# A recommender tower on one core: the first stage rearranged, and three lookups of the second quarter done ahead of the first product

## The chip, the cores and the metric

The kernel runs on one core of a Trainium2 chip. The metric is the device time of one execution in microseconds (us). The engines are TensorE (PE, with its weight loads shown apart as PEld), VectorE (DVE), ScalarE (ACT), GpSimd (POOL) and SyncE (SP), which here only issues transfers. ACT, SP and POOL issue transfers too; those issues are shown as ACTq, SPq and POOLq.

## The reference

2048 samples. For each sample 16 rows of 16 numbers are looked up in 16 tables (e), and there is an input r_x0 of 39 x 16. Their interaction is compressed to 16 x 16 numbers, and three dense layers follow:

```
e = stack([tbl_s[ids[:, s]] for s in range(16)], axis=1)          # 2048 x 16 x 16
A  = repeat(r_x0, 16, axis=1)                                     # 2048 x 624 x 16
Bm = repeat(e, 39, axis=2).reshape(2048, 624, 16)
z  = einsum('bnh,bnd,nk,khd,kd->bkh', A, Bm, alpha, w, hv)        # 2048 x 16 x 16
h  = concat([z.reshape(2048, 256), dense_ctx])                    # 272 values
y  = relu(relu(h @ W1 + b1) @ W2 + b2) @ W3                       # 2048 x 1
```

What matters here is that the product of A and Bm needs every sample's looked-up rows, and that alpha, w and hv combine to constant coefficients that don't depend on the sample.

## The kernel before, in words

**Groups.** The samples are worked on in 8 groups of 256. For each group, ACT copies the looked-up rows into a wide layout (spread, L401), TensorE transposes it into PSUM (transpose_values, L657), VectorE multiplies it with r_x0 in five products of 128 x 2048 (L576), TensorE contracts each product with the coefficients (contract, L667), and the three dense layers of the group run on TensorE beside the next group's products (layer1 L682 and L688, layer2 L698, layer3 L707) with ACT applying the nonlinearities.

**Lookups.** Seven tables are gathered by POOL with indirect transfers (L322, 14 per group). The nine small tables are looked up with matmuls: their row number is split into a low and a high digit; VectorE compares the low digit with a column of numbers (make_onehot, L524), TensorE multiplies the one-hot matrix with the table, which is split into three bf16 parts (look_up, L627, 24 matmuls; the first three tables of the nine have 64 columns, the other six 80), and VectorE picks the row by the high digit and sums (pick_rows, L536 and L540). A unit is one table for one quarter of the samples (512, two groups). Units 0 to 8 are the first quarter, done in the prologue; units 9 to 17, the second quarter, are spread over groups 0 and 1 by units_at: two beside group 0's first product, then one, one, two, one, and one beside each of group 1's first two. One-hot matrices cover half of the samples, so units 9 to 17 use those of units 0 to 8, and units 18 to 35 need the second half's digits.

**Prologue.** SP loads the row numbers, the small tables, masks, alpha, a slot mask and the weights (L272 to L278). VectorE finds the digits; ACT stores the low digits to memory (L374) and loads them back, replicated over the partitions, in three transfers (low_h, L333). VectorE makes the pick mask (L489), multiplies alpha with a mask (spread_alpha, L507), splits the tables (L496 to L502) and multiplies the weights (L514). TensorE sums alpha over the slots (sum_alpha, L595); ACT spreads the weights and the sums into block layouts (L344, L350 to L356); TensorE makes the coefficients (make_coef, L608 and L610, for each k of 16: four small matmuls into c_ps, one into c4_ps); ACT copies them to SBUF (copy_coef, L366 and L368). In program order TensorE does sum_alpha, nine lookups, with one make_coef behind each from the fourth on, the remaining ten make_coef, and then the transposes of group 0. A float32 product shows as two matmuls in the records, so make_coef has 8 + 2.

**Dense inputs.** dense_ctx and its layer weights are loaded in four replicas by 12 transfers (L297, L298) into the not yet used second half of x0_last and into z_sb, rounded by ACT (round_dense, L384, L385) and reduced to their remainders by VectorE (split_dense, L466, L469), which stands behind the third product of group 0. Only after that may x0_last of group 1 be loaded (L288 waits for dense_low).

**What sets the order.** Each engine has one list of instructions, written out by hand, and semaphores between them. All loads named so far except low_h are in SP's list, which first waits for the digits to be in (L292), then issues x0 of group 0, dense, the layers' weights, and x0 of the later groups, each when its buffer is free.

## Time and profile before

| | |
|---|---|
| median of 3 runs | 206.78 us (206.12 to 207.69) |
| the profiled execution's own time | 207.17 us |
| its span, first to last instruction | 205.4 us |
| PE busy | 171.9 us (84%) |
| DVE busy | 149.0 us (73%) |
| POOL busy | 113.2 us (55%) |
| ACT busy | 65.1 us (32%) |
| mean granted TensorE clock | 0.950 |
| pick mask (L489), one instruction | 907 ns |
| weights multiplied (L514) | 425 ns |
| dense rounded (L384 x2, L385) | 2.0 + 0.6 us |
| x0 of a group, loaded | 2 x 512 + 1024 KB |
| dense and w1d, loaded | 8 x 128 + 4 x 64 KB |
| digits (low_h), loaded per half | 3 x 768 KB |

Times in the rows are from the span's start. The page names a group of instructions by line, engine and operation; the timeline gives start and duration, merged where the same instruction repeats, and in brackets the idle time of the engine before it with what ended it. "issue" is time in which the engine waited for nothing that the profile shows. The granted clock is 1.00 at 2.4 GHz and 0.50 at 1.2 GHz. Matmuls are pipelined, so the duration of a merged row overlaps the next by some hundredths of a microsecond.

### The profile page before, as it was taken

The numbers are of one execution on the slowest core, as the hardware profiler recorded it, in microseconds if no ns is written. First come the engines' busy times: TensorE is split into PE (matmuls) and PEld (weight loads), VectorE is DVE, ScalarE is ACT, GpSimd is POOL, SyncE is SP. The second block draws the span as 40 slices with busy tenths as digits, with TensorE's granted clock in tenths as the row PEclk, the third lists the DMA queues.
The fourth block names the chain that finished last, engine by engine and source line by source line (L and its number), as shares of the span: only waits on it lengthen the run. The fifth ranks groups of instructions, "written<-read, shape, count | busy, mean of one in ns | idle before, by whom it ended". The sixth has DMA issues, their size and how long they took to land.

```text
span 205.4 us, 5054 instructions
## 1 busy us (share of the span) xinstructions
PE 171.9 (84%) x2170; PEld 128.2 (62%) x2170; DVE 149.0 (73%) x171; ACT 65.1 (32%) x203; POOL 113.2 (55%) x119
## 2 busy tenths in 40 slices
PE   0318958998638899999967999999899899899983
PEld 0307947896425677677845677777577467477671
DVE  3798872109999979898899968866979595595000
ACT  2098000729300118216201271181117317311322
POOL 2687777777777777777777777777750000000000
PEclk9999995558996999999999999999999999999999
DMA  6495999999837992991039819800693790000000
GB/s 199 146 305 156 218 205 201 271 181 267 214 77 143 197 207 27 214 199 21 6 70 199 164 26 229 175 13 10 155 206 65 184 222 6 0 3 0 3 0 2
DMA packets 11698, 26.63 MB, mean 130 GB/s; under 512 B 3836, under 2 KB 6396, under 8 KB 9628
## 3 DMA queue, kind: packets, MB, share of 16 engines
q1 hardware_dynamic: 5356, 20.50, 45.2%
q10 hardware_dynamic: 2688, 4.76, 7.7%
q0 software_dynamic: 3632, 1.06, 4.6%
q8 instruction: 17, 0.28, 0.6%
q14 instruction: 5, 0.04, 0.1%
HBM read 26.26 MB, written 0.05 MB: 128 GB/s over the span
## 4 chain that ended last, share of the span: by engine, by line
PE 59%; DVE 26%; issue 9%; DMA 2%; ACT 1%; SPq 1%; ACTq 0%; DVEq 0%
DVE prod L576 14%; PE bank L667 13%; PE bank L688 13%; PE bank L698 12%; PE bank L627 10%; PE bank L610 4%; DVE picked L536 4%; DVE onehot L524 3%; PE bank L682 2%; PE bank L657 2%; DMA prod<-slot_mask 2%; PE bank L608 2%; DVE dense_sb L466 1%; DVE prod L498 1%; PE bank L707 1%
## 5 line engine op out<-in xcount | busy, mean ns | idle before, releaser
L322 POOL DMA_INDIRECT e_all<-tbl,ids_sb x112 | 111.7, 998 | 37.6 <-issue 33.8
L576 DVE TENSOR_TENSOR prod<-x_main,bank 128x2048 f32<-128x2048 f32 x32 | 72.2, 2279 | 17.9 <-PE bank L657 9.1
L667 PE MATMUL bank<-prod,coef 128*32 128x256 f32 x640 | 43.5, 391 | 9.0 <-DVE prod L576 8.9
L627 PE MATMUL bank<-parts,onehot 125*128 125x80 bf16 (+1 forms) x864 | 39.6, 211 | 11.6 <-DVE onehot L524 5.6
L627 PEld LDWEIGHTS bank<-parts,onehot 125*128 125x128 bf16 x864 | 37.3, 108 | 15.8 <-issue 6.0
L401 ACT ACTIVATE spread<-e_all 128x128 f32<-128x128 f32 (+3 forms) x128 | 29.0, 329 | 17.5 <-DVE e_all L540 17.2
L667 PEld LDWEIGHTS bank<-prod,coef 128*32 128x32 f32 x640 | 17.0, 110 | 23.4 <-DVE prod L576 12.7
L688 PE MATMUL bank<-z_sb,w1z_sb 128*128 128x256 f32 x128 | 30.3, 380 | 0.0
L698 PE MATMUL bank<-h_sb,w_sb 128*128 128x256 f32 x128 | 29.8, 386 | 0.7 <-ACT h_sb L411 0.7
L698 PEld LDWEIGHTS bank<-h_sb,w_sb 128*128 128x128 f32 x128 | 23.7, 190 | 6.9 <-ACT h_sb L411 3.1
L536 DVE TENSOR_TENSOR picked<-bank,pick 128x320 f32<-128x320 f32 (+1 forms) x36 | 16.7, 465 | 15.2 <-PE bank L627 15.1
L411 ACT ACTIVATE h_sb<-bank 128x512 f32<-128x512 f32 x16 | 9.6, 598 | 53.7 <-PE bank L688 53.7
L688 PEld LDWEIGHTS bank<-z_sb,w1z_sb 128*128 128x128 f32 x128 | 23.1, 189 | 2.7 <-ACT z_sb L431 0.2
L576 DVE TENSOR_TENSOR prod<-x_last,bank 128x2048 f32<-128x2048 f32 x8 | 18.2, 2278 | 0.0
L540 DVE TENSOR_REDUCE e_all<-picked 128x64 f32<-128x320 f32 (+1 forms) x36 | 16.7, 464 | 1.2
L524 DVE TENSOR_SCALAR onehot<-low_h,masks_sb 125x1024 bf16<-125x1024 f16 x36 | 16.2, 497 | 0.0
L657 PEld LDWEIGHTS bank<-ident,spread 128*128 128x128 f32 x80 | 9.5, 155 | 9.5 <-issue 9.5
L657 PE MATMUL bank<-ident,spread 128*128 128x128 f32 x80 | 15.1, 311 | 0.0
L419 ACT ACTIVATE h_sb<-bank,b_sb 128x256 f32<-128x256 f32 x16 | 6.7, 471 | 12.9 <-PE bank L698 12.9
L425 ACT ACTIVATE y_sb<-bank 128x64 f32<-128x64 f32 x8 | 1.8, 224 | 25.9 <-PE bank L707 25.9
L595 PE MATMUL bank<-prod 128*128 128x128 f32 x10 | 2.5, 434 | 8.4 <-DVE prod L507 8.4
L431 ACT ACTIVATE z_sb<-bank 128x512 f32<-128x512 f32 x8 | 4.7, 592 | 14.4 <-PE bank L667 14.4
(41 smaller groups left out, 77.2 us busy)
## 6 DMA issues: line engine op xcount, KB each, us to landing
x_main<-x_m SPq DMA_DIRECT2D x16, 512.0 KB
x_last<-x_l SPq DMA_DIRECT2D x8, 1024.0 KB
low_h<-low_dram ACTq DMA_DIRECT2D x6, 768.0 KB, 8.7
e_all<-tbl,ids_sb POOLq DMA_INDIRECT x112
x_last<-dense_t SPq DMA_DIRECT2D x8, 128.0 KB
prod<-small_tables SPq DMA_DIRECT2D x1, 672.0 KB, 4.6
w1z_sb<-w1z SPq DMA_DIRECT2D x1, 512.0 KB, 14.3
w_sb<-w SPq DMA_DIRECT2D x1, 512.0 KB, 14.3
```

Source lines behind the costliest of these rows:

```text
L322: pool.indirect_dma_start(out=e_all[:, t * E + s * D:t * E + (s + 1) * D], out_offset=None, in_=tables[s], in_offset=bass.IndirectOffsetOn ...
L401: last = act.activation(dst, src, ACT.Copy)
L411: act.activation(h1_sb[:, 2 * i:2 * i + 2, :], h1_ps[i][:, :].rearrange("p (a b) -> p a b", a=2), ACT.Relu).then_inc(h1_ready, 1)
L524: dve.tensor_scalar(onehot[:, n, c, :], low_h[0:RC, n, :], low_sb[:, c:c + 1], None, ALU.is_equal).then_inc(onehot_ready, 1)
L536: dve.tensor_tensor(found, look_ps[i % 2][:, 0:QT * q * D].rearrange("p (t d q) -> p t d q", t=QT, q=q), pick[:, at:at + QT, 0:q].unsqueez ...
L540: dve.tensor_reduce(e_all[:, :].rearrange("p (t i) -> p t i", i=E)[:, u * QT:(u + 1) * QT, s * D:(s + 1) * D], found, AX_X, ALU.add).then_ ...
L576: dve.tensor_tensor(prod[:, c, :, :], x0[:, p, :, :], value_bank(g, c // 2)[:, c % 2 * GB:(c % 2 + 1) * GB].unsqueeze(1).broadcast_to([P, ...
L627: last = pe.matmul(look_ps[i % 2][:, t * w:(t + 1) * w], onehot[:, n, c, at:at + P], parts[:, part, col:col + w], start=(t == 0 and c == 0 ...
L657: last = pe.transpose(value_bank(g, i)[:, col:col + P], spread[:, p, t, c * P:(c + 1) * P], ident[:, :])
L667: last = pe.matmul(z_ps[p][32 * q:32 * q + 32, a * GB:(a + 1) * GB], coef[:, c, 4 * a + q, :], prod[:, c, 4 * a + q, :], start=(c == 0 and ...
L688: last = pe.matmul(out[a], w1z_sb[:, k, cols[a]], z_sb[:, p, k, :], start=False, stop=(k == 1), skip_group_check=True)
L698: last = pe.matmul(out[a], w2_sb[:, c, cols[a]], h1_sb[:, c, :], start=(c == 0), stop=(c == N1 // P - 1))
```

## The change

- SP's first loads are reordered: masks, weights, alpha, slot mask, and the small tables last.
- The loads of low_h move from ACT's list to SP's; the second half's stand behind x0 of group 1 instead of behind round_dense on ACT.
- The dense loads stand ahead of x0 of group 0; round_dense on ACT stands ahead of the spread of group 0, and split_dense on VectorE behind the first quarter's lookups, ahead of the first product.
- VectorE multiplies the weights first, then spreads alpha, then makes the pick mask, then splits the tables.
- make_coef is cut in two: main_coef (c_ps) and last_coef (c4_ps). TensorE makes eight main parts ahead of the first lookup, one behind each of the other eight, and two last parts behind each lookup from the fourth on, the remaining four behind the ninth.
- Units 9, 10 and 11 are looked up and picked ahead of group 0's first product instead of in group 0.

```diff
--- before.py
+++ after.py
@@ -98,9 +98,10 @@
 
 RUNS = spread_runs()
 FIRST_COLS = COL0[3]
-COEF_FROM, DENSE_AT = 3, 2
+COEF_FROM = 3
 
 UNITS_AT = (2, 1, 1, 2, 1, 1, 1)
+AHEAD = 3
 LAYER1_AT, LAYER2_AT = (0, 1), 2
 
 
@@ -109,7 +110,8 @@
     first, at = NSMALL * (step // (2 * NC) + 1), step % (2 * NC)
     if first >= 4 * NSMALL or at >= len(UNITS_AT):
         return range(0)
-    return range(first + sum(UNITS_AT[:at]), first + sum(UNITS_AT[:at + 1]))
+    done = max(AHEAD, sum(UNITS_AT[:at])) if step < 2 * NC else sum(UNITS_AT[:at])
+    return range(first + done, first + max(done, sum(UNITS_AT[:at + 1])))
 
 
 def gathered_by(g):
@@ -270,12 +272,21 @@
         @block.sync
         def _(sp):
             sp.dma_start(ids_i, ids_d).then_inc(digits_in, 16)
-            sp.dma_start(table_sb, small_tables).then_inc(table_in, 16)
             sp.dma_start(masks_sb[:, :], masks).then_inc(masks_in, 16)
+            sp.dma_start(w_hv_sb[:, :], w_hv.unsqueeze(0).broadcast_to([J, D, K * H + K])).then_inc(coef_in, 16)
             sp.dma_start(alpha_sb[:, :, :], alpha.rearrange("(c p) k -> p c k", p=P)).then_inc(prep_in, 16)
             sp.dma_start(mask_sb, slot_mask).then_inc(prep_in, 16)
-
-            sp.dma_start(w_hv_sb[:, :], w_hv.unsqueeze(0).broadcast_to([J, D, K * H + K])).then_inc(coef_in, 16)
+            sp.dma_start(table_sb, small_tables).then_inc(table_in, 16)
+
+            def load_low(a, n, count):
+
+                sp.dma_start(low_h[:, n:n + count, :], low_dram[n:n + count, a * HALF:(a + 1) * HALF].unsqueeze(0).broadcast_to(
+                    [P, count, HALF])).then_inc(low_in[n // 3], 16)
+
+            sp.wait_ge(low_stored, 16)
+            for n in range(0, NSMALL, 3):
+                load_low(0, n, 3)
+
             def load_x0(g, p):
 
                 if g >= 2:
@@ -290,16 +301,20 @@
 
             for n in range(NSMALL // 3):
                 sp.wait_ge(low_in[n], 16)
-            load_x0(0, 0)
             for q in range(4):
                 rows = slice(32 * q, 32 * q + 32)
                 for a in range(2):
                     sp.dma_start(dense_f[a][rows, :], dense_t[:, a * HALF:(a + 1) * HALF]).then_inc(dense_in, 16)
                 sp.dma_start(w1d_f[rows, :], w1d).then_inc(dense_in, 16)
+            load_x0(0, 0)
             sp.dma_start(w1z_sb[:, :, :], w1z.rearrange("(a p) n -> p a n", p=P)).then_inc(mlp_in, 16)
             sp.dma_start(w2_sb[:, :, :], w2.rearrange("(a p) n -> p a n", p=P)).then_inc(mlp_in, 16)
             sp.dma_start(w3_sb[:, :], w3).then_inc(mlp_in, 16)
-            for g in range(1, GROUPS):
+            load_x0(1, 1)
+            sp.wait_ge(onehot_ready, 2 * NSMALL)
+            for n in range(0, NSMALL, 3):
+                load_low(1, n, 3)
+            for g in range(2, GROUPS):
                 load_x0(g, g % 2)
             sp.wait_ge(y_ready, GROUPS)
             sp.dma_start(y.rearrange("(g q b) a -> q g (b a)", g=GROUPS, q=4), y_sb[0:97:32, :, :]).then_inc(stored, 16)
@@ -327,11 +342,6 @@
         @block.scalar
         def _(act):
 
-
-            def load_low(a, n, count):
-
-                act.dma_start(low_h[:, n:n + count, :], low_dram[n:n + count, a * HALF:(a + 1) * HALF].unsqueeze(0).broadcast_to(
-                    [P, count, HALF])).then_inc(low_in[n // 3], 16)
 
             act.wait_ge(warm_ready, 1)
             act.activation(warm[:, 1:2], warm[:, 0:1], ACT.Copy)
@@ -361,7 +371,7 @@
 
             def copy_coef():
 
-                act.wait_ge(c_done, 1)
+                act.wait_ge(c_done, 2)
                 for h in range(2):
                     act.activation(coef[:, 0:MC, :, h * K:(h + 1) * K].rearrange("p c a k -> p (c a) k"),
                                    c_ps[:, :].rearrange("p (k c) -> p c k", k=K), ACT.Copy, scale=half_sb[:, h:h + 1])
@@ -372,9 +382,6 @@
 
             act.wait_ge(low_ready, 1)
             act.dma_start(low_dram.rearrange("n b -> (n b)").rearrange("(p c) -> p c", p=P), low16[:, :]).then_inc(low_stored, 16)
-            act.wait_ge(low_stored, 16)
-            for n in range(0, NSMALL, 3):
-                load_low(0, n, 3)
             spread_weights()
             spread_sums()
 
@@ -431,13 +438,10 @@
                 act.activation(z_sb[:, p, :, :], z_ps[p][:, :].rearrange("p (a b) -> p a b", a=2),
                                ACT.Copy).then_inc(z_ready, 1)
 
+            round_dense()
             act.wait_ge(pads_done, 1)
             spread_group(0, 0)
             copy_coef()
-            round_dense()
-            act.wait_ge(onehot_ready, 2 * NSMALL)
-            for n in range(0, NSMALL, 3):
-                load_low(1, n, 3)
             for g in range(GROUPS):
                 p = g % 2
                 for c in range(NC):
@@ -544,12 +548,12 @@
             find_digits()
             pads = spread[:, :, :, MC * P:EXW].rearrange("p a t (h c) -> p (a t) h c", h=2)
             dve.memset(pads[:, :, :, (F - FM) * J - 1:64], 0.0).then_inc(pads_done, 1)
+            multiply_weights()
+            spread_alpha()
             make_pick()
-            spread_alpha()
             dve.wait_ge(table_in, 16)
             split_tables(0, slice(0, FIRST_COLS))
             dve.wait_ge(split_step, 4)
-            multiply_weights()
             split_tables(1, slice(FIRST_COLS, W))
             make_onehot(0)
             dve.wait_ge(pick_ready, 1)
@@ -558,6 +562,9 @@
                 if n < NSMALL - 1:
                     make_onehot(n + 1)
                 pick_rows(n)
+            split_dense()
+            for i in range(NSMALL, NSMALL + AHEAD):
+                pick_rows(i)
             for i in units_at(0):
                 if i // NSMALL % 2 == 0:
                     make_onehot(i)
@@ -571,14 +578,12 @@
                     if g > 0:
                         dve.wait_ge(contracted, NC * (g - 1) + (c + 1))
                     if g == 0 and c == 3:
-                        dve.wait_ge(c_done, 1)
+                        dve.wait_ge(c_done, 2)
                     x0 = x0_main if c < MC else x0_last
                     dve.tensor_tensor(prod[:, c, :, :], x0[:, p, :, :],
                                       value_bank(g, c // 2)[:, c % 2 * GB:(c % 2 + 1) * GB].unsqueeze(1).broadcast_to(
                                           [P, HP, GB]), ALU.mult).then_inc(product_ready, 1)
 
-                    if g == 0 and c == DENSE_AT:
-                        split_dense()
                     for i in units_at(NC * g + c):
                         pick_rows(i)
                     for i in units_at(NC * g + c + 1):
@@ -596,17 +601,18 @@
                                      alpha_block[:, c, :, :].rearrange("p f k -> p (f k)"), start=True, stop=True)
                 last.then_inc(bsum_done, 1)
 
-            def make_coef(k):
-
-                if k == 0:
-                    pe.wait_ge(bsum_copied, 2)
-                    pe.wait_ge(wblock_done, 1)
-                    pe.wait_ge(blast_done, 1)
+            def main_coef(k):
+
                 for j in range(2):
                     for odd in range(2):
                         row = 64 * j + 32 * odd
-                        pe.matmul(c_ps[row:row + FM, k * MC * HP:(k + 1) * MC * HP], bsum_sb[:, 0:FM, k],
-                                  wblock[:, k, j::2, odd::2], start=True, stop=True)
+                        last = pe.matmul(c_ps[row:row + FM, k * MC * HP:(k + 1) * MC * HP], bsum_sb[:, 0:FM, k],
+                                         wblock[:, k, j::2, odd::2], start=True, stop=True)
+                if k == K - 1:
+                    last.then_inc(c_done, 1)
+
+            def last_coef(k):
+
                 last = pe.matmul(c4_ps[:, k * H:(k + 1) * H], blast[:, k, :, :, :].rearrange("p h f j -> p (h f j)"),
                                  wh_sb[:, k, :], start=True, stop=True)
                 if k == K - 1:
@@ -629,18 +635,29 @@
                                              stop=(c == 1 and part == PARTS - 1), skip_group_check=True)
                 last.then_inc(onehot_used, 1)
 
+            sum_alpha()
+            pe.wait_ge(bsum_copied, 2)
+            pe.wait_ge(wblock_done, 1)
+            for k in range(K - NSMALL + 1):
+                main_coef(k)
+            pe.wait_ge(split_step, 4)
             made = 0
-            sum_alpha()
-            pe.wait_ge(split_step, 4)
             for n in range(NSMALL):
                 if n == 3:
                     pe.wait_ge(split_step, 8)
                 look_up(n)
+                if n > 0:
+                    main_coef(K - NSMALL + n)
+                if n == COEF_FROM:
+                    pe.wait_ge(blast_done, 1)
                 if n >= COEF_FROM:
-                    make_coef(made)
-                    made += 1
+                    for k in range(made, made + 2):
+                        last_coef(k)
+                    made += 2
             for k in range(made, K):
-                make_coef(k)
+                last_coef(k)
+            for i in range(NSMALL, NSMALL + AHEAD):
+                look_up(i)
 
             def transpose_values(g, i):
```

## Rows read from the trace of the kernel before

**Rows 1.** Chain of waits, 24 to 46 us: start, duration, what.
```profile
24.53 0.27 PE bank L608 x8
24.80 0.33 PE bank L610 x2
...
28.46 3.23 issue
...
43.27 0.29 PE bank L608 x7
43.55 0.54 PE bank L610 x2
```

**Rows 2.** Transfer queues, 28 to 30 us: queue, packets, MB, share of 16 engines.
```profile
q8 instruction: 1, 0.02, 3.9%
```

**Rows 3.** Windows: length, PE, PEld, DVE, ACT, POOL busy, PEclk, DMA share, GB/s.
```profile
30.00:40.00 10.00, 8.31 (x115) 7.52 (x115) 1.96 (x4) 3.00 (x13) 7.55 (x8) 0.56 1.06 227
40.00:50.00 10.00, 9.91 (x135) 8.31 (x136) 3.93 (x6) 5.41 (x14) 7.56 (x8) 0.59 1.00 211
```

**Rows 4.** Timeline of TensorE: start, duration, instruction, idle before.
```profile
15.33 2.72 PE L627 MATMUL bank<-parts,onehot 125*128 125x64 bf16 x48 [4.42 <-DVE onehot L524]
...
24.98 1.02 PE L627 MATMUL bank<-parts,onehot 125*128 125x80 bf16 x24
...
34.07 1.76 PE L627 MATMUL bank<-parts,onehot 125*128 125x80 bf16 x24
...
44.30 0.61 PE L610 MATMUL bank<-wh_sb,prod 128*128 128x16 f32 x2
44.75 1.95 PE L657 MATMUL bank<-ident,spread 128*128 128x128 f32 x8
...
62.25 1.93 PE L667 MATMUL bank<-prod,coef 128*32 128x256 f32 x16 [1.68 <-DVE prod L576]
```

**Rows 5.** Timeline of VectorE.
```profile
7.46 0.82 DVE L507 TENSOR_TENSOR prod<-alpha_sb,masks_sb 128x640 f32<-128x640 f32 x1
...
14.30 1.67 DVE L524 TENSOR_SCALAR onehot<-low_h,masks_sb 125x1024 bf16<-125x1024 f16 x4
...
36.40 0.49 DVE L540 TENSOR_REDUCE e_all<-picked 128x64 f32<-128x320 f32 x1
45.98 2.29 DVE L576 TENSOR_TENSOR prod<-x_main,bank 128x2048 f32<-128x2048 f32 x1 [9.10 <-PE bank L657]
...
49.87 2.28 DVE L576 TENSOR_TENSOR prod<-x_main,bank 128x2048 f32<-128x2048 f32 x1
...
55.16 2.36 DVE L466 TENSOR_TENSOR dense_sb<-x_last,dense_sb 64x1024 fp32r<-64x1024 f32 x2
57.56 1.40 DVE L469 TENSOR_TENSOR w1d_sb<-z_sb,w1d_sb 32x512 fp32r<-32x512 f32 x2
...
67.14 2.28 DVE L576 TENSOR_TENSOR prod<-x_main,bank 128x2048 f32<-128x2048 f32 x1
```

**Rows 6.** Timeline of ACT.
```profile
10.77 3.30 ACT L344 ACTIVATE prod<-wh_sb,masks_sb 128x256 f32<-128x256 f32 x8 [8.53 <-DVE wh_sb L514]
...
37.00 3.62 ACT L401 ACTIVATE spread<-e_all 128x128 f32<-128x128 f32 x16 [17.22 <-DVE e_all L540]
...
49.40 3.62 ACT L401 ACTIVATE spread<-e_all 128x128 f32<-128x128 f32 x16 [0.26 <-DMA e_all<-tbl,ids_sb]
...
170.86 3.61 ACT L401 ACTIVATE spread<-e_all 128x128 f32<-128x128 f32 x16
```

**Rows 7.** Timeline of SP's issues.
```profile
18.32 1.15 SPq L285 DMA_DIRECT2D x_main<-x_m  x2
...
26.35 0.44 SPq L299 DMA_DIRECT2D w1z_sb<-w1z  x1
```

**Rows 8.** Issues by line, section 6: count, KB each, us from issue to landing.
```profile
w1z_sb<-w1z SPq DMA_DIRECT2D x1, 512.0 KB, 14.3
```

**Rows 9.** Timeline of POOL, its last gather.
```profile
151.16 0.95 POOL L322 DMA_INDIRECT e_all<-tbl,ids_sb  x1 [0.30 <-issue]
```

## The prediction

> **What bounds the kernel now.** I read the views in this order: the critical chain over the prologue, TensorE's and VectorE's timelines over the same stretch, the clock of its second half, then the queues that feed it.
>
> The chain from 24 to 45 us lies almost wholly on TensorE [rows 1]. At 28.46 us it stands still for 3.23 us and waits for nothing that the profile shows ("issue"), in the middle of a lookup. In that gap the queue of kind "instruction" moves its first packet [rows 2]. I read the stall as TensorE waiting for code. After it the granted clock is 1.2 GHz (0.56 and 0.59 as means of the two stretches), although TensorE is busy 8.31 and 9.91 us of 10 [rows 3]. One coefficient k (four small products into c_ps, then one with a 128x128 weight into c4_ps) costs 0.27 + 0.33 us before the stall and 0.29 + 0.54 us behind it [rows 1]. A lookup of the 80-column kind takes 1.02 us before it and 1.7 us behind it, one of the 64-column kind 1.36 us at the low clock; the transposes that end the prologue take 1.23 us until the first product can start (44.75 to 45.98) [rows 4, 5].
>
> VectorE finishes the first quarter's last lookup at 36.9 us and then idles 9.1 us until its first product at 45.98; what it waits for is TensorE, which works off the last coefficients until 44.9 [rows 4, 5]. ACT's spread of group 0 (37.00 to 40.6) is under that cover [rows 6]. So **the prologue is bound by TensorE**. In group 0, from 45.98 to 67.14, it is the other way round: VectorE alternates products and lookups without a gap and holds 3.76 us of split_dense as well [rows 5]. **Group 0 is bound by VectorE.** From there on the groups run on their own chains and would follow rigidly.
>
> **The change, part by part.**
>
> *VectorE's first tasks.* The order becomes weights, alpha, pick, table. The alpha product starts at 7.46 now, held by a load [rows 5]; the table no longer stands ahead of that load, so I take 7.0, and the pick mask (0.9 in the profile table) now stands behind it, while the weights (0.42) have moved ahead. The first one-hot starts at 14.5 instead of 14.30. Bounds: 14.2 to 15.3.
>
> *Coefficients.* TensorE idles until its first lookup at 15.33 [rows 4]. The weights reach ACT before 7 us instead of at 10.77, so its 3.30 us of spreading end before sum_alpha, and the copies of the sums at about 11.5 [rows 6]. The first eight main parts, 8 x 0.29 = 2.3 us, then fall in idle time. The other eight and sixteen last parts go between or behind the lookups; cover for those is gone once TensorE is the later engine.
>
> *The stall comes earlier.* TensorE had executed 10 + 7 x 24 + 4 x 10 + 1 = 219 matmuls (sum_alpha, seven lookups, four coefficients, the first of lookup 7) when it ran dry. In the new order the 219th is the 21st of the 24 in lookup 4: 10 + 64 (eight main parts of 8) + 24 + 3 x 32 + 4 (two last parts of 2) + 21. I charge the same 3.2 us there. Bounds: nothing, if a wait for VectorE covers it, to 3.2.
>
> *The clock.* From the stall's end at 31.69 to 44.9 the rows show 13 us of nearly unbroken work at 1.2 GHz, most of it coefficients [rows 1, 3]. The new stream behind the stall is again lookups mixed with coefficients, more of them per lookup (0.29 + 2 x 0.54 against 1.7 us). So I take the low clock up to the first product. The Trainium skill, "TensorE: Matmul & The Clock Gate", section "What's actually happening", says: "the default state is throttled, and activity releases the throttle." By that, denser work would lift the clock; the trace disagrees for this mix, and what the rule would give is rival 1.
>
> *The sum up to the first product,* all at the low clock. Lookup 0: 15.5 to 16.9. Lookup 1 with a main part: 18.8. Lookup 2: 20.4. Lookup 3 with main and two last parts, 1.7 + 0.29 + 1.08 = 3.07: 23.5. Lookup 4 meets the stall: 25.0, 28.2, done with its coefficients at 29.8. Lookups 5 to 7: 3 x 3.07, 39.0; lookup 8 ends at 40.7. VectorE (0.87 one-hot and 0.97 pick per lookup) is below 3.07 and doesn't count. The coefficients that are left, 0.29 + 6 x 0.54: 44.2. Now three more lookups of 64 columns, 3 x 1.36: 48.3. Transposes 1.23: **49.5**, and VectorE's pick of the third ends at 49.2, so the first product starts at 49.4 instead of 45.98: **+3.4**.
>
> Beside it on VectorE: split_dense from 41.7 to 45.5, then the picks of lookups 9 and 10 (0.8 each), so lookup 11's wait for pick 9 (45.9) ends before TensorE gets there (46.9). ACT: spread 41.8 to 45.4, coefficients copied by 47.5; both covered.
>
> *Group 0.* It loses split_dense, 3.76, and three picks of 0.8 each (two of them are 48.27 to 49.87) [rows 5]: 6.16. The picks that stay now wait for a lookup that TensorE starts only after a contraction; I charge 0.2. 21.16 - 6.0 = 15.2: **-6.0**. Group 1 then starts at 64.6 instead of 67.14.
>
> *The transfers.* SP takes over the loads of the digits, three issues of some 0.5 us, and issues them when the store has landed, as ACT did. From 18.32 it queues dense and w1d (1.28 MB) ahead of x0 of group 0 (2 MB) [rows 7]. What was queued up to w1z (3.8 MB) had landed by 26.35 + 14.3 = 40.65 [rows 7, 8], an estimated 0.17 MB/us: dense by 26, ACT's 2.7 us of rounding by 29, x0(0) by 38, or by 40.65 at the latest; needed at 41.7 and 49.4. Cost 0; if dense came only at 40.65 it would be 1 us. The second half's digits are now queued behind x0_last of group 1, which waits for split_dense (45.5); before they were issued at 45: 3.3 MB, at 0.17 to 0.22 MB/us in by 61 to 65, needed at about 78. Cost 0. Behind them on SP stands x0(2), which waits for group 0's last product (63) anyway.
>
> *Later stages.* The last gather of group 1 lands at 49.4, where ACT waits 0.26 us for it now [rows 6]; its spread then ends at 53, and TensorE asks for it at about 60. The last gather of all is issued at 151.2 [rows 9] against a spread at 170.9 [rows 6]. An earlier start of 3 to 9 us is hidden from both.
>
> Sum: +3.4 - 6.0 = -2.6 against the profiled execution's own 207.17: 204.6. That execution is 0.39 above the median of 206.78, so **204.2** on the scale of the median.
>
> **Rivals.**
>
> 1. *The clock rises behind the stall.* For it: lookups leave fewer gaps, and at 24.98 a lookup ran at 2.4 GHz. Against it: 13 us at 1.2 GHz behind the present stall. Price: 29.2 after lookup 4, 1.0 + 0.27 + 0.66 = 1.93 per lookup, lookup 8 ends at 36.0, split_dense at 40.9, the third lookup ahead at 42.2, its pick at 43.3. The first product starts at 43.3: -2.7 - 6.0 = -8.7, **198.1**. If it rises halfway, about 201.
>
> 2. *The clock falls in group 0.* It would be slower. TensorE has too little to do between the transposes and the second contraction, and the clock drops as it did around the 1.68 us gap in the present group 0, behind which a contraction took 1.93 us [rows 4]. Then lookup 12 ends at 58.2, the next two with their contraction at 65.4, transposes 66.5, lookup 15 68.2, its pick 69.2. Price: 69.2 - 67.14 = +2.1, **208.9**. It decides once the clock stays low past lookup 12; a single contraction at the low clock costs under 1 us, since VectorE covers it. If two last parts in a row cost 0.61 each (as the last record of them shows), 1.1 more.
>
> 3. *The gain in group 0 doesn't show*, because the prologue pays all of it: last parts at 0.61 (+1.1), the first one-hot at 15.3 (+0.8), dense late (+1.0). **206.8**, no change.
>
> Excluded: the change not doing what it says. The three lookups and split_dense stand in program order ahead of the first product on both engines.
>
> **The numbers.** The forecast's case has a chance of 0.58 (202.5 to 206), rival 1 with its halfway form 0.20, rival 2 0.10, rival 3 0.12. A measurement tells 1% (2.1 us) from no change: bounds 204.7 and 208.8. Faster by over 1%: 0.20 and six tenths of the forecast's 0.58 make 0.55. Slower by over 1%: half of rival 2 and a rest for a second stall, 0.10. Within: 0.35. The range leaves out the further half of rival 1, and rival 2: 199.0 to 207.2.
>
> **What would show it.** First one-hot at 14.5; an "issue" stall of about 3.2 us on TensorE near 25 us; lookup 8 ending at 40.7 with a granted clock near 0.5 in 30 to 40 us; first product at 49.4, group 1's first at 64.6, from there the same distances to the end. A first product at 43 to 45 with a clock near 1 is rival 1; gaps of VectorE ahead of picks in group 0 are rival 2. A product of group 0 waiting for x0, or a one-hot of the second half waiting for its digits, would prove the transfers wrong.

## The result and the profile after

The changed kernel takes 201.01 us (median of 4 runs, 200.01 to 201.94), the kernel before 206.45 us beside it; the ratio is 0.9725 with a 95% interval of 0.966 to 0.9791. The forecast was 204.2 in a range of 199.0 to 207.2: the time lies in the range and the direction is right, but the gain is twice the one forecast, and it came about in another way than the sum says. The profiled execution took 201.36 us with a span of 199.6. Where a version's slowest executions lie more than 1.5% above its fastest (one each of e2, e3, e5, e8 and e12, two of e13, seven of e9), its ratio in the table below leaves them out and its median counts them.

The clock and the busy time in the prologue, from the windows of the changed kernel; columns as in [rows 3]:

```profile
20.00:30.00 10.00, 9.59 (x208) 8.81 (x204) 9.83 (x24) 0.98 (x2) 7.56 (x9) 1.00 0.76 189
30.00:40.00 10.00, 6.73 (x124) 6.11 (x120) 7.61 (x14) 6.81 (x23) 7.87 (x8) 0.84 1.01 217
40.00:50.00 10.00, 7.03 (x96) 4.08 (x97) 8.34 (x6) 0.00 (x0) 7.56 (x9) 0.65 1.07 225
50.00:60.00 10.00, 5.08 (x72) 3.74 (x69) 5.48 (x6) 3.58 (x16) 7.56 (x9) 0.86 1.06 297
```

From 20 to 30 us TensorE and VectorE both work almost without a gap, at 2.4 GHz (granted clock 1.00). The stall of [rows 1] is gone. TensorE's timeline:

```profile
15.93 2.72 PE L633 MATMUL bank<-parts,onehot 125*128 125x64 bf16 x48 [3.70 <-DVE onehot L528]
...
29.83 1.02 PE L633 MATMUL bank<-parts,onehot 125*128 125x80 bf16 x24
30.78 0.33 PE L609 MATMUL bank<-prod,bsum_sb 128*32 128x32 f32 x8
31.04 1.51 PE L616 MATMUL bank<-wh_sb,prod 128*128 128x16 f32 x12
32.40 1.56 PE L633 MATMUL bank<-parts,onehot 125*128 125x64 bf16 x48
36.24 1.02 PE L633 MATMUL bank<-parts,onehot 125*128 125x64 bf16 x24 [2.28 <-DVE picked L540]
37.07 1.95 PE L674 MATMUL bank<-ident,spread 128*128 128x128 f32 x8
```

Lookup 8 ends at 30.8 us (35.8 before), the last coefficient at 32.4 (44.9 before). VectorE's timeline, to be read against [rows 5]:

```profile
37.78 0.42 DVE L544 TENSOR_REDUCE e_all<-picked 128x64 f32<-128x256 f32 x1
40.53 6.68 DVE L583 TENSOR_TENSOR prod<-x_main,bank 128x2048 f32<-128x2048 f32 x3 [2.33 <-DMA x_last<-x_l]
...
53.27 2.28 DVE L583 TENSOR_TENSOR prod<-x_last,bank 128x2048 f32<-128x2048 f32 x1
60.45 0.49 DVE L540 TENSOR_TENSOR picked<-bank,pick 128x320 f32<-128x320 f32 x1 [4.90 <-PE bank L633]
...
61.38 2.28 DVE L583 TENSOR_TENSOR prod<-x_main,bank 128x2048 f32<-128x2048 f32 x1
...
170.84 8.88 DVE L583 TENSOR_TENSOR prod<-x_main,bank 128x2048 f32<-128x2048 f32 x4 [4.16 <-issue]
```

The first product starts at 40.53 (45.98 before) and has waited 2.33 us for x0_last. Group 1's first product starts at 61.38 (67.14 before), behind an idle time of 4.90 us. So group 0 takes 20.85 us from first product to first product, against 21.16 before. The last group starts 5.82 us earlier (170.84 against 176.66), as much as group 1 and as the span: nothing is won or lost behind group 1.

What holds group 1 is in the chain of waits of the changed kernel:

```profile
42.78 0.30 issue
43.09 10.96 DMA e_all<-tbl,ids_sb
54.04 0.02 issue
54.06 1.39 ACT spread L408 x5
55.46 0.05 issue
55.51 2.14 ACT spread L408 x11
57.65 0.04 issue
57.70 0.48 PE bank L674
```

Group 1's last gather is issued at 43.09 and lands 10.96 us later; before, it was issued at 43.98, and ACT waited 0.26 us for it, until 49.40 [rows 6]. This is a new wait, and it took the place of VectorE's work as the bound of group 0.

### The profile page after: what moved, and what is told of

It is laid out like the page before. It is cut to its first block, busy times and chain, and to the rows that moved or that the text cites. A ratio compares the mean times of both kernels' runs of the same rounds, so it can differ in the third digit from the quotient of the medians.

```text
span 199.6 us, 5054 instructions
## 1 busy us (share of the span) xinstructions
PE 165.2 (83%) x2170; PEld 121.8 (61%) x2170; DVE 149.0 (75%) x171; ACT 65.2 (33%) x203; POOL 112.8 (57%) x119
## 4 chain that ended last, share of the span: by engine, by line
PE 51%; POOL 15%; DVE 13%; issue 9%; DMA 7%; ACT 3%; DVEq 0%; POOLq 0%
POOL e_all L337 15%; PE bank L684 14%; PE bank L705 13%; PE bank L715 12%; DVE prod L583 10%; PE bank L633 6%; DMA e_all<-tbl,ids_sb 5%; PE bank L674 3%; PE bank L699 3%; ACT spread L408 2%; DMA ids_sb<-ids 2%; DVE picked L540 2%; DVE onehot L528 1%; PE bank L724 1%; ACT h_sb L426 0%
## 5 line engine op out<-in xcount | busy, mean ns | idle before, releaser
L684 PE MATMUL bank<-prod,coef 128*32 128x256 f32 x640 | 45.3, 398 | 9.7 <-DVE prod L583 9.6
L633 PE MATMUL bank<-parts,onehot 125*128 125x80 bf16 (+1 forms) x864 | 36.0, 204 | 7.3 <-DVE onehot L528 5.0
L633 PEld LDWEIGHTS bank<-parts,onehot 125*128 125x128 bf16 x864 | 33.9, 102 | 10.4 <-DVE parts L506 3.8
L684 PEld LDWEIGHTS bank<-prod,coef 128*32 128x32 f32 x640 | 17.8, 112 | 25.8 <-DVE prod L583 9.8
L699 PE MATMUL bank<-dense_sb,w1d_sb 128*128 128x256 f32 x32 | 8.0, 331 | 0.3 <-ACT y_sb L432 0.3
## 6 DMA issues: line engine op xcount, KB each, us to landing
low_h<-low_dram SPq DMA_DIRECT2D x6, 768.0 KB, 15.2
```

Source lines behind the costliest of these rows:

```text
L633: last = pe.matmul(look_ps[i % 2][:, t * w:(t + 1) * w], onehot[:, n, c, at:at + P], parts[:, part, col:col + w], start=(t == 0 and c == 0 ...
L684: last = pe.matmul(z_ps[p][32 * q:32 * q + 32, a * GB:(a + 1) * GB], coef[:, c, 4 * a + q, :], prod[:, c, 4 * a + q, :], start=(c == 0 and ...
L699: pe.matmul(out[a], w1d_sb[:, cols[a]], dense_sb[:, m * GB:(m + 1) * GB], start=(a == 0), stop=False, skip_group_check=True)
```

## The experiments

Each set of runs has runs of the kernel before beside it, on the same chip (medians 206.45, 207.02, 207.27 and 206.94 us), and each ratio is to those; so versions are compared by their ratios. "x0(1)" is x0 of group 1, and "e5 + ..." is e5 with one wait more.

| kernel | median us | ratio, 95% interval | first product | gathers of group 1 in | group 1 starts |
|---|---|---|---|---|---|
| before | 206.45 | 1 | 45.98 | 49.40 | 67.14 |
| the change | 201.01 | 0.9725 (0.966 to 0.9791) | 40.53 | 54.06 | 61.38 |
| e1 before, loads late | 209.99 | 1.0171 (1.0131 to 1.0211) | 41.48 | 53.11 | 67.06 |
| e9 before, coefficients alone | 206.27 | 0.9742 (0.9686 to 0.9798) | 39.55 | 50.38 | 62.59 |
| e11 before, lookups ahead alone | 207.77 | 1.0036 (1.0008 to 1.0063) | 48.44 | 50.91 | 67.14 |
| e3 change, no lookups ahead | 197.79 | 0.9551 (0.952 to 0.9583) | 42.73 | 51.78 | 59.76 |
| e4 change, x0 before dense | 205.65 | 0.9941 (0.9913 to 0.9969) | 49.33 | 48.56 | 65.35 |
| e10 change, split_dense in group 0 | 203.78 | 0.987 (0.9813 to 0.9926) | 41.95 | 49.39 | 61.29 |
| e2 change, digits after the gathers | 199.01 | 0.9614 (0.9547 to 0.9681) | 41.32 | 50.95 | 58.07 |
| e5 change, own semaphore for x0_last | 199.26 | 0.9652 (0.9579 to 0.9725) | 39.53 | 51.96 | 58.10 |
| e7 e5 + x0_last(1), digits after the gathers | 196.66 | 0.947 (0.9413 to 0.9528) | 38.28 | 50.15 | 56.65 |
| e8 e7, no lookups ahead | 196.89 | 0.9485 (0.9427 to 0.9542) | 37.70 | 50.35 | 56.50 |
| e12 e5 + all of x0(1) after the gathers | 196.82 | 0.9489 (0.9431 to 0.9548) | 38.81 | 44.71 | 54.50 |
| e13 e5, digits before x0(1) | 201.61 | 0.9659 (0.9597 to 0.9721) | 45.52 | 48.01 | 61.78 |

The last three columns are from the profiled execution of each (for the gathers: when ACT's spread of group 1 starts, which in all of them ends a wait for the gathers).

**The stall.** e1 holds the loads of x0 of group 0 and all behind them until lookup 4 is done (about 25 us instead of 18.3):

```diff
             for n in range(NSMALL // 3):
                 sp.wait_ge(low_in[n], 16)
+            sp.wait_ge(onehot_used, 5)
             load_x0(0, 0)
```

> The kernel before, with one wait more on SP: x0 of group 0, dense and all that stands behind them are issued only when lookup 4 is done (about 25 us) instead of at 18.3. Theory A (the 3.2 us stall at 28.46 is a code fetch that stood behind the x0 loads on the transfer engines): the first code packet moves near 20 to 23 us instead of at 28.77, no issue gap over 1 us on TensorE before 30 us, lookup 8 ends near 31 instead of 35.8, first product near 39 to 41 instead of 45.98; time 199 to 202. Theory B (the stall comes from the place in the program where TensorE's code runs out, whatever the transfers do): the stall of about 3.2 us stays at 28.5 and the time is 205 to 208.

The stall at 28.46 is gone, and the kernel is 1.7% slower: theory A was right on the code packet and wrong on the time. The packets of the "instruction" queue by windows, in e1 one from 22 to 24 and another, with the same line, from 34 to 36 us (none between):

```profile
q8 instruction: 1, 0.02, 4.0%
```

The first packet now moves at 22 to 24 us, where x0 isn't yet in flight, instead of at 28 to 30 [rows 2]. The second one falls under x0's loads, and there is a stall of 1.85 us instead, ahead of a coefficient:

```profile
36.66 0.35 PE L609 MATMUL bank<-prod,bsum_sb 128*32 128x32 f32 x8 [1.85 <-issue]
```

The first product comes 4.5 us earlier, but everything loaded behind x0 is late: dense, x0_last of group 1 (VectorE waits 3.47 us for it ahead of group 1). Group 1 starts at 67.06 as before. Behind that wait TensorE has been idle for 4.18 us and its granted clock is down; e1, then the kernel before:

```profile
70.00:74.00 4.00, 4.00 (x22) 2.73 (x15) 2.47 (x2) 0.00 (x0) 3.08 (x4) 0.60 0.94 187
70.00:74.00 4.00, 4.00 (x58) 3.05 (x54) 2.93 (x3) 0.60 (x1) 3.01 (x4) 1.00 0.98 198
```

VectorE then waits 2.69 us for the next lookup, where it waited 1.07 before, and these 1.6 us make up the difference of the two spans (206.9 and 205.4).

e9 is the kernel before with the coefficients' part alone (SP's first six loads, weights first on VectorE, main_coef and last_coef; dense, x0, digits and units 9 to 11 as before):

```diff
+            pe.wait_ge(bsum_copied, 2)
+            pe.wait_ge(wblock_done, 1)
+            for k in range(K - NSMALL + 1):
+                main_coef(k)
+            pe.wait_ge(split_step, 4)
...
+                if n > 0:
+                    main_coef(K - NSMALL + n)
...
                 if n >= COEF_FROM:
-                    make_coef(made)
-                    made += 1
+                    for k in range(made, made + 2):
+                        last_coef(k)
+                    made += 2
```

> The kernel before with the coefficients' part of the change alone: SP's first six loads reordered, weights and alpha first on VectorE, main_coef and last_coef split, eight main parts ahead of the lookups. Dense, x0, digits and the three lookups as before. Theory A (the prologue was held by TensorE's coefficients and by the late code packet; eight main parts early bring the first 256 instructions ahead of the x0 loads): first code packet near 19.5, no stall of 3 us before 30, first product at 37 to 41, 199.5 to 202, so most of the change's gain. Theory B (the gain comes from the order of the transfers and the dense part): stall near 25 to 28, first product at 44 to 46, 204 to 207.

Its ten runs fall into two bunches, 201.4 to 202.6 (three) and 205.4 to 209.2 (seven). The profiled execution is of the first bunch; what makes the second slower is not shown by any trace. Its chain:

```profile
29.31 0.17 PE bank L628 x4
29.48 2.48 issue
31.96 1.51 PE bank L628 x20
```

TensorE runs the same program up to here as in the change, at the same pace, but x0's loads are in flight from 21 us on, and its second code packet moves between 29 and 30 us, not between 24 and 25 as in the change. It stalls 2.48 us. The change has no such stall: in it the dense loads are in flight at that time.

Counted in program order, as the prediction does, TensorE runs dry behind its 219th matmul in the kernel before and in e11 (2.73 us), and behind its 346th in e9 and in e1. So there are places at which code runs out, here 127 matmuls apart, and whether TensorE stands still there depends on whether the packet has come. In the change the first two packets move at 19 to 20 and at 24 to 25 us, and TensorE reaches the two places at about 23.5 and 30. TensorE goes on up to some 3 us after the packet has moved (28 to 29 and 31.69 before, 29 to 30 and 31.96 in e9, about 35 and 36.66 in e1); what takes this time the profile doesn't show.

What x0's loads do to small packets shows in the queues. The kernel before, 20 to 28 us, x0 in flight:

```profile
DMA packets 301, 1.76 MB, mean 220 GB/s; under 512 B 57, under 2 KB 88, under 8 KB 88
...
q1 hardware_dynamic: 245, 1.75, 97.6%
q0 software_dynamic: 56, 0.02, 1.8%
```

The changed kernel in the same stretch, dense in flight (q0 holds the gathers):

```profile
DMA packets 762, 1.37 MB, mean 172 GB/s; under 512 B 282, under 2 KB 379, under 8 KB 761
...
q1 hardware_dynamic: 571, 1.31, 62.4%
q0 software_dynamic: 190, 0.05, 6.4%
```

Of 301 packets before, 213 are of 8 KB and more, and the gathers get 56 through; of 762 after, one is, and they get 190 through. The "instruction" queue has the same neighbours. That the code packet comes late under x0's loads and in time elsewhere is shown by the kernels before, e1, e9 and the change (e4 and e11 agree); that the size of the packets does it, rather than the load of 97.6% against 62.4%, is not told apart by these.

e4 turns the order of x0 and dense back in the change:

```diff
+            load_x0(0, 0)
             for q in range(4):
...
-            load_x0(0, 0)
```

> The changed kernel with x0 of group 0 issued ahead of the dense loads, as before the change; nothing else moved. Theory A (x0's arrival at 40.5 sets the first product; transfers of 2 MB right behind the digits also delay code fetches): x0 is in by 32, but dense lands 7 to 10 us later, ACT's rounding ends near 39 to 41, and since the spread of group 0 stands behind it the first product comes at 44 to 46; a code fetch near 24 us is late by 3 to 5 us, perhaps with a stall; time 202 to 206. Theory B (the order of these two loads doesn't matter): 200 to 202.

Theory A was right on the order, and the first product came later still. ACT waits 24.24 us for the dense loads and rounds until 42.4, split_dense ends at 46.3, the first product comes at 49.33 (44 to 46 expected). In the profiled execution VectorE's picks of lookups 4 to 8 are 2.85 us apart, the pace of 1.2 GHz (below); the second code packet again moved at 29 to 30 us, but at that pace TensorE reached its 346th matmul only at about 35.5. So within the change the order "dense, then x0" is worth 4.6 us of the 5.4; here the rounding stands ahead of the spread and split_dense ahead of the first product, so late dense loads hold both, which they didn't in the kernel before.

**What the three lookups are worth.** e11 adds them alone to the kernel before:

```diff
+AHEAD = 3
...
+            for i in range(NSMALL, NSMALL + AHEAD):
+                look_up(i)
```

> The kernel before with AHEAD = 3 alone: three lookups between the last coefficient and the first transposes, all else as before. Theory A (the three lookups delay the first product by about what they take out of group 0): first product at 48.5 to 50 instead of 45.98, group 1's first product 1 us earlier to 2 us later than 67.14, 206 to 209. Theory B (they are a gain of 2.4 us): 204 to 205.

As theory A said: first product at 48.44 instead of 45.98 (+2.46), group 1 at 67.14, the same hundredth as before; the time is 0.4% longer. e3 takes them out of the change:

```diff
-AHEAD = 3
+AHEAD = 0
```

> The changed kernel with AHEAD = 0: no lookup ahead of the first product, units 9 to 11 back in group 0. Theory A (the start of group 1 is held by the gather, not by VectorE's work in group 0, so moving the three lookups bought nothing): first product still at 40.5 (held by x0), group 1's first product at 60.5 to 62, time within 0.5% of the change (200 to 202). Theory B, the prediction's (every us taken out of group 0 on VectorE comes off the time): 2.4 us slower than the change, 203 to 204.

Both theories missed: it is faster than the change, 0.9551 against 0.9725, intervals apart. Its first product comes 2.2 us later, yet group 1 starts at 59.76, with no gap on VectorE ahead of it, since the gathers are in at 51.78 instead of 54.06. Its x0_last of group 1 and its digits are issued at 41.6 to 43.8 in the profile, 4 to 6 us later than the change's. That profile is of a run of 199.93; of the other four, three took 197.5 to 197.8 and one 202.0. In it TensorE ran the lookups at the pace that 1.2 GHz has in [rows 4], without a gap:

```profile
29.13 1.76 PE L633 MATMUL bank<-parts,onehot 125*128 125x80 bf16 x24
30.82 0.36 PE L609 MATMUL bank<-prod,bsum_sb 128*32 128x32 f32 x8
31.11 1.03 PE L616 MATMUL bank<-wh_sb,prod 128*128 128x16 f32 x4
31.98 1.76 PE L633 MATMUL bank<-parts,onehot 125*128 125x80 bf16 x24
```

The same instructions take 1.02, 0.33 and 0.62 us in the change's profile. (The windows of this execution give a granted clock of 1.00 over its whole span, and those of before do so for the slow lookups from 15 us on. So that it is the clock is an inference from the durations and is not shown by the clock's own rows.) TensorE's program up to lookup 8 is the same in the change and in all versions of it. Of these ten profiled executions seven ran lookups 4 to 8 at 1.02 us each, and three (e3, e4, e13) at 1.76. e8 takes them out of e7:

> e7 with AHEAD = 0, the three lookups back in group 0. Once the gather no longer holds group 1, VectorE's work in group 0 should count: if the prediction's reason for moving the lookups holds then, 1 to 2.5 us slower than e7. If the lookups ahead delay the first product by as much as they take out of group 0, the same as e7 within 0.7 us.

The same within 0.7 us, as the second theory said. In no version are the three lookups a gain.

**VectorE's load in group 0.** e10 puts split_dense back behind the third product:

```diff
-            split_dense()
             for i in range(NSMALL, NSMALL + AHEAD):
                 pick_rows(i)
...
+                    if g == 0 and c == 2:
+                        split_dense()
```

> The changed kernel with split_dense back behind the third product of group 0 (the dense loads and ACT's rounding stay early). Theory A (VectorE has 4.9 us of idle time ahead of group 1, so 3.8 us more in group 0 cost nothing; and x0_last of group 1 and the digits, which wait for split_dense, now leave the transfer engines to the gathers): the gathers of group 1 land at 48 to 51 instead of 54, group 1's first product at 57 to 61, 198 to 201. Theory B, the prediction's (VectorE's work in group 0 is on the path): 3 to 4 us slower than the change, 204 to 205.

Theory A is right up to group 1 and wrong behind it. With 3.8 us more in group 0, group 1 starts at 61.29, where the change's starts at 61.38; the gathers are in at 49.39. But x0_last of group 1 and the digits wait for split_dense, so they are late (issued at 52.5 to 54.9), x0 of group 2 behind them too, and VectorE's timeline has this wait ahead of group 2:

```profile
79.99 2.29 DVE L582 TENSOR_TENSOR prod<-x_main,bank 128x2048 f32<-128x2048 f32 x1 [3.05 <-DMA x_last<-x_l]
```

The early split_dense pays, 2.8 us, through the loads that it releases and not through VectorE.

**The gathers.** e2 holds the digits back until the gathers of group 1 are in:

```diff
             sp.wait_ge(onehot_ready, 2 * NSMALL)
+            sp.wait_ge(gathered[1], gathered_by(1))
             for n in range(0, NSMALL, 3):
                 load_low(1, n, 3)
```

> The changed kernel, with one wait more on SP: the second half's digits (3 x 768 KB) are issued only when the gathers of group 1 have landed. Theory A (these loads delay group 1's last gather, which lands at 54.04, 11 us after its issue, and this holds the spread, the transposes and lookup 15): the spread of group 1 starts at 46 to 49, group 1's first product at 56 to 57.5 instead of 61.4; time 196 to 197.5. Theory B (x0 of group 1 and the gathers' own small packets hold it, the digits don't): the spread starts at 52 to 54 as now and the time stays at 200 to 202. If the digits come too late instead, a one-hot in front of group 2 waits, near 72 us, and the time is 201 or more.

Between the two: the gathers land 3.1 us earlier, group 1 starts at 58.07, and the time is 199.01; against the change its interval overlaps. e5 gives x0_last its own semaphore:

```diff
+                    if c == MC:
+                        dve.wait_ge(x0_last_in[p], 16 * (g // 2 + 1))
```

> The changed kernel; x0_last gets semaphores of its own, so the first four products of a group no longer wait for it. Theory A (group 1 starts when the last gather of group 1 has landed, wherever group 0 starts): first product at 38 to 39 instead of 40.5, but VectorE's gap ahead of group 1 grows by as much, group 1's first product at 60.5 to 61.5, time within 0.5% of the change (200 to 202). Theory B (an earlier first product goes straight to the end): 2 us faster, 198.5 to 199.5.

The first product moved by 1.0 us, group 1 by 3.3, because the gathers landed 2.1 us earlier in this profile, with the same loads in flight. Most of that is that POOL issued the last one earlier, at 41.38 instead of 43.09; from there it took 10.55 us, against 10.96. So the landing differs by 2 us between executions, and differences of landings below that tell nothing. Against the change e5's ratio is lower by 0.007, inside the intervals. e7 holds back x0_last of group 1 too, e12 all of x0 of group 1:

```diff
                 if g == 1:
                     sp.wait_ge(dense_low, 4)
+                    sp.wait_ge(gathered[1], gathered_by(1))      # e7
...
+            sp.wait_ge(gathered[1], gathered_by(1))              # e12, not e7
             load_x0(1, 1)
```

> e5 with one wait more on SP: x0_last of group 1 and the second half's digits are issued only when the gathers of group 1 have landed. Theory A (the gathers' small packets are held up by the 8 KB packets of x0_last as well as by the digits): the gathers land at 45 to 48, the spread of group 1 starts there, group 1's first product at 54.5 to 56.5, if the later loads are then in time for group 2 (needed near 70) 194 to 196; if x0 of group 2 is late, up to 199. Theory B (they are late for another reason, such as their own number): spread of group 1 at 50 or later, 198 to 200.

> e5 with one wait more on SP: all of x0 of group 1 (8 KB packets) and the digits behind it are issued only when the gathers of group 1 have landed. Theory A (small gather packets stand behind 8 KB packets of x0_main as well): the gathers, whose last issue is at about 43, land at 45 to 47 instead of 50 to 54; spread of group 1 there. The transfers then have 6.3 MB to bring from 45 us on, at 0.2 MB/us until 76, so x0 of group 2 is late: 196 to 201. Theory B (the gathers are late by themselves): landing at 50 or later and 200 to 205.

In e7 the gathers land at 50.15, at the edge of theory B, behind x0_main (1 MB, the only large load of group 1 that is still ahead of them); the time, 196.66, is better than theory B's. In e12 almost nothing else is in flight from 42 us on (0.02 MB of loads from 42 to 44), and they land at 44.71, ACT's timeline:

```profile
44.71 3.65 ACT L410 ACTIVATE spread<-e_all 128x128 f32<-128x128 f32 x16 [6.71 <-DMA e_all<-tbl,ids_sb]
```

That is theory A of e12: without the loads of group 1 the gathers land 5 to 9 us earlier. From the issue of the last one it is 3.4 us in e12 (41.28 to 44.71), 8.1 in e7, 10.6 in e5 and 11.0 in the change. It doesn't bring more than e7, since the loads held back are missing later; VectorE in e12, ahead of group 2:

```profile
73.44 2.29 DVE L587 TENSOR_TENSOR prod<-x_main,bank 128x2048 f32<-128x2048 f32 x1 [3.28 <-DMA x_main<-x_m]
```

e13 sends the same bytes in another order, the digits (2 KB packets) ahead of x0 of group 1 (8 KB):

```diff
-            load_x0(1, 1)
             sp.wait_ge(onehot_ready, 2 * NSMALL)
             for n in range(0, NSMALL, 3):
                 load_low(1, n, 3)
+            load_x0(1, 1)
```

> e5 with the digits (2 KB packets) ahead of x0 of group 1 (8 KB packets): the same bytes in flight while the gathers of group 1 run, only the packet size differs. Theory A (the size of the neighbour's packets sets the gathers' delay): they land at 45 to 48; then x0_main of group 1 is late (57 to 59) and holds group 1, 198 to 201. Theory B (only the bytes in flight count): landing at 50 to 54 as in e5, and group 1 at 58 to 60.

The gathers land at 48.01 with the digits in flight, at the early edge of what x0's packets give (48.56 to 54.06) and well behind 44.71. From the issue of the last one it is 5.8 us, against 10.6 in e5. That is inconclusive on packet size: the profiled execution ran its lookups at the pace of 1.2 GHz and its first product came 6 us later, so the two aren't alike. Its four runs spread from 198.8 to 203.9.

## Why the prediction was right, and where it was wrong

The direction was right, and so was the reason for a part of it: the prologue was held by TensorE, and its coefficients could be moved into idle time. That the time fell into the range is in good part luck, since two large errors of opposite sign met in it. Three steps failed: the stall, the clock, and the end of group 0.

*VectorE's first tasks.* Right: alpha at 6.64, the first one-hot at 14.91 (14.5 forecast, bounds 14.2 to 15.3); ACT's spreading of the weights at 6.18, the eight main parts at 10.94 in idle time.

*"The stall comes earlier. I charge the same 3.2 us there."* **The first step that failed.** I took it for a point in the program at which the code runs out, counted to it, and kept its length. The points exist (the 219th matmul, and the 346th in e1 and e9), but TensorE stands still there only when the code packet is late, and it is late when it has to get past x0's loads: the first packet moved at 28 to 29 us before and at 19 to 20 in the change; the second at 24 to 25 in the change and at 29 to 30 with x0 first (e4, e9). There was no stall in the change. I had the packet's row [rows 2] and that of x0's issue at 18.32 [rows 7], and didn't put them together. My own bound "nothing, if a wait covers it" had the size right for the wrong reason. Size: 3.2 us.

*"I take the low clock up to the first product."* **The second, and the largest.** Wrong in the profiled execution of the change, where lookups 3 to 8 took 1.02 us each, at a granted clock of 1.00. From the start of lookup 3 to the end of lookup 8 I had 17.1 us without the stall, and it took 9.8; the last coefficients took 1.6 instead of 3.5. Size: 7.3 + 1.9 us. On the clock it was my rival 1 that came, priced at 198.1 with a chance of 0.20. It isn't wrong in all executions: in e3's profile the same instructions ran at the pace of 1.2 GHz, 2.85 us per lookup, with TensorE busy from 20.6 us on. The sentence of the Trainium skill, "TensorE: Matmul & The Clock Gate", section "What's actually happening", "the default state is throttled, and activity releases the throttle", fits the change's profile and not e3's, where 19 us of work nearly without a gap kept the slow pace. What decides between the two paces is open. So the clock of this stretch could not be forecast as one number; both belonged in the range.

*The first product.* 49.4 forecast, 40.53 measured; rival 1 said 43.3, with the stall still in. The 8.9 us are made up of 3.2 (stall), 7.3 (lookups 3 to 8) and 1.9 (coefficients), less 0.6 (lookup 3 started at 21.01, not at 20.4), 0.6 (the three lookups ahead took 4.7, not 4.1, with a wait of 2.28 for a pick in them) and 2.3 (the wait for x0_last, which now holds the first product). Dense was in at 29.0 and rounded by 31.5, 3 us later than forecast, and that cost nothing. "x0(0) by 38, or by 40.65 at the latest" was right as a time; "cost 0" held only against a first product at 49.4. A cover that is priced by one's own late forecast has to be priced again when the forecast moves.

*Group 0, "-6.0".* **The third.** 20.85 against 21.16 us, so -0.3. The work did leave VectorE: its last product of group 0 ends 15.0 us after the first one starts. But then it waits 4.90 us for a lookup that stands behind the transposes of group 1, those for ACT's spread, and that for the gathers. I had named this wait (49.4, "its spread then ends at 53, and TensorE asks for it at about 60") and left the landing at its old time, while the same change moved x0_last and the digits on top of it. I had not asked what the earlier split_dense triggers: it ended at 35.7, SP issued 1 MB and 2.3 MB behind it, and the gathers stood under them. VectorE's own share was forecast well: in e12, where the gathers come in time, group 0 takes 15.7 us from first product to first product (38.81 to 54.50), and 15.2 were forecast.

*Later stages* shifted rigidly, as forecast: 5.76 us at group 1, 5.82 at the last.

So +3.4 - 6.0 = -2.6 became -5.45 - 0.3 = -5.8. Two errors of opposite sign, the first by -8.9 and the second by +5.7, left 3.2: the total is nearer than either term. A smaller slip: rival 3's three costs add up to 2.9, so its price is 207.1 and not 206.8.

What the parts are worth, as far as it is shown: the coefficients' part alone gives nearly the whole gain in three of ten runs (201.4 to 202.6) and little or nothing in the others (205.4 to 209.2); dense ahead of x0 is worth 4.6 us within the change (e4) and the early split_dense 2.8 (e10); the three lookups nothing in the kernel before and in e7, and in the change they cost 3.2 us by the medians (e3). Why they cost that much there is open; that the gathers land later with them rests on one profile each, and the landing differs by 2 us from run to run.

The best version measured is e7, 196.66 us, ratio 0.947; e8 and e12 can't be told from it.

## What to carry to other kernels

A stall in which an engine waits for nothing visible is to be laid beside the transfer queues: if the "instruction" queue moves a packet just then, look at what else is in flight; here reordering the loads moved the packet and removed the stall. A tail of small gathers needs the transfer engines free of large loads at the moment when it is waited for, not on average; a load that a change sets free earlier lands on top of it. And work moved off a busy engine is worth only as much as the next wait allows: in a sum of two terms, the second has to be worked out again whenever the first one moves.

## What the runs showed of the hardware

With the loads of x0 and the digits of group 1 in flight the last of its gathers took 10.96 us from issue to landing; with almost nothing else in flight (e12) it took 3.4 us (41.28 to 44.71). The same stretch of TensorE's program ran at 2.4 GHz in one execution (the change) and at the pace of 1.2 GHz, from 20.6 to 39.5 us with hardly a gap, in another (e3); what that costs was not measured alone, since x0_last holds the first product in the change. One code packet is 0.02 MB; when it moved 5 to 6 us later under x0's loads than without them, TensorE stood still for 2.5 us (e9, against the change) and 3.2 us (before, against e1).
